# A step's piece between the two score pairs of its unit, in a fused attention kernel

## The chip, the cores and the metric

The kernel runs on one core of a Trainium2 chip. The metric is the device time of one execution in microseconds. The kernel before was run three times: 4042.91, 4030.77 and 4035.91 us, median 4035.91 us. One further execution was profiled.

## The reference

The input x has 4 batches of 2048 tokens of 256 features. Per batch:

```
h = layernorm(x) * (1 + ca) + sa
q, k = h @ Wq.T, h @ Wk.T            # 32 score heads of 8 features
v = h @ Wv.T                         # 16 value heads of 16 features
aw = softmax(q k^T * 8**-0.5)        # 32 heads, each 2048 x 2048
attn = (aw[even head] - lam * aw[odd head]) @ v
attn = rmsnorm(attn) * subln_w * (1 - LAMBDA_INIT)
x = x + ga * (attn @ Wo.T)
h = layernorm(x) * (1 + cb) + sb
x = x + gb * (h @ (ternary weight * scale).T)
```

Every element of every softmax has to go through one exponential: 4 x 32 x 2048 x 2048 of them. They are the bulk of the work.

## The kernel before

**The main loop.** It has 16 bodies, four per batch. A body covers 8 score heads (two groups of four) over all 2048 queries, in 128 units. A unit is one block of 128 keys against 512 queries for the four heads of a group. Sixteen units (all key blocks) make a segment, so a body has 8 segments. The loop has 2048 units.

**A unit on each engine.** TensorE computes the scores of a unit in two pairs of heads, numbers n = 2u and 2u+1 (`scores`, line 730). A pair is two matmuls, each with 64 contraction rows in one half of the array and 128 x 512 results, into one of three slots of two PSUM banks (`SLOTS = 3`). Before it, TensorE waits until ScalarE has finished the exponentials of pair n-3, which held the slot. ScalarE runs one ACTIVATE (Exp) of 128x1024 per pair (line 630), and does nothing else in the main loop. Two units later (`LAG = 2`) TensorE multiplies the exponentials with the values (`weighted`, line 744): four fp32 matmuls side by side in column tiles 32 wide, all 128 rows, shown in the trace as x8. They accumulate in one bank over the 16 units of a segment.

**Behind a segment.** VectorE transposes that bank into SBUF (line 994), then normalises the result in a chain of small instructions with a power by GpSimd in the middle (line 604). The first `weighted` of the next segment waits until the transpose has read the bank (`pv_read`).

**Steps and pieces.** The projections before the attention (kind "a", 8 steps for 512 tokens), the output projection and the second layer behind it (kind "e", 6 steps) and the bounds of the softmax ("m") of other batches are threaded through the units of a body, by a table that `steps_of` makes by hand. A step of kind a or e is cut into four pieces, one piece in a unit. A piece is four column-tiled fp32 matmuls, 128 columns each where it transposes (line 650) or 256 columns each where it projects (lines 656 and 664). `spread` puts the four pieces of a step in units 1, 3, 5 and 7 of a half segment, so a run of steps has a piece in every second unit. `close` puts them in four units in a row. All steps share one PSUM bank (`aux`). So the first piece of a step waits until VectorE has evacuated the step before it, and some wait for more: step 2 of kind e waits for `e_normed`, the normalised rows that VectorE (with a power on GpSimd) makes from steps 0 and 1; step 0 of kind e waits for its loads (`e_loaded`).

**Order on TensorE.** It executes in program order. In every unit it issues the scores of pair 2u, those of pair 2u+1, the weighted sum of unit u-2, and then, if the table has one, the piece.

**The tables by size.** Bodies 0 to 3 (batch 0) have the 8 steps of kind a only. Bodies 4 to 11 also have the 6 steps of kind e. Bodies 3, 7 and 11, the last of their batch, use close runs from segment 3 on (`A_TURN`, `E_TURN`, `M_TURN`); all else in bodies 0 to 11 is spread. Bodies 12 and 13 have two jobs of kind e each, spread. Body 15 has 14 steps of kind e, all close (`E_LAST`). After the main loop 10 steps of kind e are done whole.

Of the kernel before, what the change touches and what calls it, by code (L numbers as in the profile page):

```python
# [37 lines left out]
def adaln_diff_attention(nc, x, wqT, wkT, wvT, woT, lq1, lk1, lq2, lk2, subln, wfT, cT, wmod, out):  # L38
# [11 lines left out]
    PAIRS = 2  # L50
# [24 lines left out]
    A_STEPS, E_STEPS = 8, 6  # L75


    PIECES = 4
# [3 lines left out]
    M_STEPS = M_BOUNDS + NC + 1  # L82
# [59 lines left out]
    DMA = 16  # L142
# [8 lines left out]
    with ExitStack() as ctx:  # L151
# [105 lines left out]
        aux = ps[:, 7, :]  # L257
# [21 lines left out]
        a_normed = sem("a_normed")  # L279
        a_product = sem("a_product")  # L280
        a_evacuated = sem("a_evacuated")
# [352 lines left out]
        def _(pe):  # L634
# [70 lines left out]
            def m_step(m, i, bank=aux):  # L705

                if i == 0:
                    pe.wait_ge(m_open, m + 1)
                if i < M_BOUNDS:
                    for blk in range(M_BLOCKS * i, min(M_BLOCKS * (i + 1), NB)):  # L710
                        for c in range(EC):
                            at = (blk % M_BLOCKS) * (NS * BOX) + c * (NS // EC) * BOX
                            for sign in range(2):
                                last = nc.tensor.matmul(bank[:, at:at + (NS // EC) * BOX], q_sign[:, c, sign, blk * P:(blk + 1) * P],
                                                        box_w[:, c, sign, :, :].rearrange("p h k -> p (h k)"), start=(sign == 0), stop=(sign == 1))
                elif i < CRIT:
                    pe.wait_ge(m_split_done, m + 1)
                    last = m_transposes(i - M_BOUNDS, bank)
                else:
                    pe.wait_ge(m_crit_done, m + 1)  # L720
                    last = nc.tensor.transpose(bank[0:1, 0:P], m_crit[:, 0:1], ident[:, :])
                last.then_inc(m_product, 1)

            def scores(body, u, n):

                (buf, tc), blk = place_of(body, u // NB), u % NB
                pe.wait_ge(exp_done, body * (2 * BODY) + n + 1)
                for half in range(2):
                    at = 64 * half
                    last = nc.tensor.matmul(slots[slot_of(body, n)][:, half, :], keys[buf][at:at + KS_ROWS, n % PAIRS, blk * P:(blk + 1) * P],  # L730
                                            queries[buf][at:at + KS_ROWS, n % PAIRS, tc * CH:(tc + 1) * CH], start=True, stop=True)
                last.then_inc(scores_ready, 1)

            def weighted(body, u):
# [10 lines left out]
                                                start=(blk == 0), stop=(blk == NB - 1))  # L745
                last.then_inc(pv_done, 1)

            for tc in range(NC):
                for i in range(A_STEPS):
                    if i == 0:  # L750
                        pe.wait_ge(a_normed, tc + 1)
                    elif i == 2:
                        pe.wait_ge(a_evacuated, tc * A_STEPS + 2)
                    for p in range(PIECES):
                        last = a_piece(i, p, ps[:, i, :])
                    last.then_inc(a_product, 1)
# [7 lines left out]
            for b in range(B):  # L764
                pe.wait_ge(m_flag_set, b + 1)
                exact = pe.value_load(m_flag[0:1, 0:1], min_val=0, max_val=1)
                pe.reg_mov(behind, 1)
                with pe.If(exact > 0):

                    if b > 0:  # L770
                        for u in range(BODY - LAG, BODY):
                            weighted(b * GP - 1, u)
                    pe.reg_mov(behind, 0)

                    runs = pe.snap(exact_runs, min_val=0, max_val=B - 1)
                    pe.wait_ge(m_evacuated, (b + 1) * M_STEPS)
                    pe.wait_ge(pv_read, b * (GP * SEGS) + 1)
                    with pe.Fori(0, NG) as g:
                        pe.wait_ge(m_rows_loaded, (runs * EXACT_LOADS + (g + 1) * ROW_LOADS) * DMA)
                        for n in range(4 * NB):  # L780
                            head, blk = n // NB, n % NB
                            pair, at = head // 2, 64 * (head % 2)
                            pe.wait_ge(m_reduced, (runs * NG + g) * (4 * NB) + n + 1)
                            for k in range(NC):
                                last = nc.tensor.matmul(ps[:, 4 * (n % 2) + k, :], queries[0][at:at + KQ, pair, blk * P:(blk + 1) * P],
                                                        keys[0][at:at + KQ, pair, k * CH:(k + 1) * CH], start=True, stop=True)
                            last.then_inc(m_scores, 1)
                    wait_alone(pe, m_reduced, (runs + 1) * NG * (4 * NB) + 2, pe_passed)
                    wait_alone(pe, exact_split, runs + 1, pe_passed)
                    for k in range(NC):  # L790
                        if k > 0:
                            pe.wait_ge(exact_evacuated, runs * NC + k)
                        m_transposes(k, aux).then_inc(exact_product, 1)
                    wait_alone(pe, exact_evacuated, (runs + 1) * NC, pe_passed)
                    wait_alone(pe, m_rows_loaded, (runs + 1) * (EXACT_LOADS * DMA), pe_passed)
                    pe.reg_add(exact_runs, exact_runs, 1)

                for gp in range(GP):
                    body = b * GP + gp
                    steps, before = steps_of(body), None  # L800
                    for u in range(BODY):
                        if u % NB == 0 and place_of(body, u // NB)[1] == 0:
                            pe.wait_ge(group_loaded[place_of(body, u // NB)[0]], (body + 1) * (GROUP_LOADS * DMA))
                        for n in (PAIRS * u, PAIRS * u + 1):
                            scores(body, u, n)
                        if u >= LAG:
                            weighted(body, u - LAG)
                        elif gp > 0:
                            weighted(body - 1, BODY - LAG + u)
                        elif b > 0:  # L810
                            with pe.If(pe.snap(behind, min_val=0, max_val=1) > 0):
                                weighted(body - 1, BODY - LAG + u)
                        if u not in steps:
                            continue
                        kind, job, i, p = steps[u]
                        if before and (kind == "m" or p == 0):

                            bkind, bjob, bi = before
                            if bkind == "a":
                                pe.wait_ge(a_evacuated, bjob * A_STEPS + bi + 1)  # L820
                            elif bkind == "e":
                                pe.wait_ge(e_evacuated, bjob * E_STEPS + bi + 1)
                            else:
                                pe.wait_ge(m_evacuated, bjob * M_STEPS + bi + 1)
                        before = (kind, job, i)
                        if kind == "m":
                            m_step(job, i)
                        elif kind == "a":
                            if i == 0 and p == 0:
                                pe.wait_ge(a_normed, job + 1)  # L830
                            elif i == 2 and p == 0:
                                pe.wait_ge(a_evacuated, job * A_STEPS + 2)
                            last = a_piece(i, p, aux)
                            if p == PIECES - 1:
                                last.then_inc(a_product, 1)
                        else:
                            if i == 0 and p == 0:
                                pe.wait_ge(e_evacuated, job * E_STEPS)
                                pe.wait_ge(e_loaded, (job + 1) * 3 * DMA)
                            elif i == 2 and p == 0:  # L840
                                pe.wait_ge(e_normed, job + 1)
                            elif i == 4 and p == 0:
                                pe.wait_ge(e_evacuated, job * E_STEPS + 4)
                            last = e_piece(i, p, aux)
                            if p == PIECES - 1:
                                last.then_inc(e_product, 1)
            for u in range(BODY - LAG, BODY):
                weighted(B * GP - 1, u)

# [313 lines left out]
```

## Time and profile before

| | us |
|---|---|
| median of three runs | 4035.91 |
| the profiled execution | 4034.29 |
| its span, from the first to the last instruction | 4032.6 |
| ScalarE busy in the span | 3783.3 (94%) |
| TensorE busy in the span | 3766.2 (93%) |
| VectorE busy | 1199.4 (30%) |
| GpSimd busy | 635.7 (16%) |

The granted TensorE clock is 0.98 of full speed as a mean over the span. A busy share of TensorE counts modelled ends of matmuls, which overlap the next instruction, so it overstates the engine's load; the starts of instructions are the safer reading.

### The profile page before, as it was taken

The page shows a single profiled execution, that of the slowest core. Times are in us where ns is not written, and L with a number is a line of the kernel's source. Part 1 is how long each engine was busy: PE and PEld are TensorE (multiplying, and loading weights), DVE is VectorE, ACT ScalarE, POOL GpSimd, SP SyncE. Part 2 cuts the span into 40 slices and gives each one's busy share as a digit, 9 for nine tenths or more (in the row PEclk, how much of TensorE's full clock was granted, in tenths as well). Part 3 has the DMA queues.
Part 4 walks back from the last instruction along what each step waited for, and adds up shares of the span by engine and source line. Part 5 has one row for each costly group of instructions (what it writes and reads, how often), then busy time and mean ns, then how long its engine had stood idle before and what let it go on. Part 6 is the DMA issues. An engine that isn't in the chain of part 4 may idle for free.

```text
span 4032.6 us, 75553 instructions
## 1 busy us (share of the span) xinstructions
PE 3766.2 (93%) x32082; PEld 944.9 (23%) x32082; DVE 1199.4 (30%) x2778; ACT 3783.3 (94%) x4132; POOL 635.7 (16%) x402
## 2 busy tenths in 40 slices
PE   6599999999999999999999999999999999999897
PEld 3122212222222222222222222222222222211122
DVE  7222322223332323233323232232332222211134
ACT  1599999999999999999999999999999999999895
POOL 4111211111121211212012121211201001001011
PEclk8799999999999999999999999999999999999999
DMA  3402121210232323023231222222012220211101
GB/s 127 86 25 34 36 41 36 44 29 25 35 53 40 53 37 48 29 35 51 43 48 29 43 40 46 47 44 45 25 34 37 41 40 14 43 19 25 35 19 40
DMA packets 113773, 163.25 MB, mean 40 GB/s; under 512 B 19012, under 2 KB 88388, under 8 KB 113224
## 3 DMA queue, kind: packets, MB, share of 16 engines
q1 hardware_dynamic: 113416, 158.19, 21.3%
q8 instruction: 260, 4.26, 0.5%
q14 instruction: 97, 0.79, 0.1%
HBM read 97.82 MB, written 60.32 MB: 39 GB/s over the span
## 4 chain that ended last, share of the span: by engine, by line
ACT 50%; issue 22%; PE 20%; DVE 3%; DMA 2%; SPq 1%; POOL 1%; POOLq 0%; DVEq 0%; ACTq 0%
ACT probs L630 50%; PE ps L744 10%; PE ps L730 6%; PE ps L656 2%; PE ps L664 1%; SPq L383 1%; DMA queries<-m_scr 1%; DVE normed L872 1%; DVE stats L861 0%; PE ps L650 0%; POOL seg_rs L604 0%; DMA e_x<-in_x_dram 0%; POOL e_rstd L580 0%; DVE e_tmp L980 0%; DMA m_scr<-wmod_sb 0%
## 5 line engine op out<-in xcount | busy, mean ns | idle before, releaser
L630 ACT ACTIVATE probs<-ps 128x1024 f32<-128x1024 f32 x4096 | 3762.6, 1452 | 112.6 <-PE ps L730 111.4
L744 PE MATMUL ps<-probs,values 128*32 128x512 f32 x16384 | 2195.8, 608 | 7.9 <-DVE seg_t L994 3.1
L730 PE MATMUL ps<-queries,keys 64*128 64x512 bf16 x8192 | 1465.8, 387 | 142.2 <-DMA queries<-m_scr 44.0
L604 POOL TENSOR_TENSOR seg_rs<-seg_ms,neg_half 64x16 f32<-64x16 f32 x128 | 370.4, 2894 | 2967.6 <-DVE seg_ms L1003 2967.6
L730 PEld LDWEIGHTS ps<-queries,keys 64*128 64x128 bf16 x8192 | 370.5, 93 | 1874.8 <-ACT probs L630 1575.7
L744 PEld LDWEIGHTS ps<-probs,values 128*32 128x32 f32 x16384 | 323.1, 108 | 588.1 <-issue 516.4
L994 DVE STREAM_TRANSPOSE seg_t<-ps 128x512 f32<-128x512 f32 x128 | 91.8, 717 | 902.6 <-PE ps L744 902.6
L980 DVE TENSOR_TENSOR e_tmp<-ps,e_gate 128x512 f32<-128x512 f32 x64 | 44.1, 689 | 468.0 <-PE ps L656 468.0
L1007 DVE TENSOR_TENSOR seg_n<-seg_d,seg_rs 64x256 f32<-64x256 f32 x128 | 62.8, 490 | 386.5 <-POOL seg_rs L604 386.5
L957 DVE TENSOR_SCALAR a_qk<-ps 128x512 f32<-128x512 f32 x64 | 44.2, 691 | 347.5 <-PE ps L664 347.2
L650 PE MATMUL ps<-ident,normed 128*32 128x128 f32 x2048 | 99.4, 284 | 49.9 <-DVE normed L872 38.7
L1011 DVE SCALAR_TENSOR_TENSOR seg_a<-seg_n,subln_sb 32x256 f32<-32x256 f32 x256 | 133.8, 523 | 6.1
L650 PEld LDWEIGHTS ps<-ident,normed 128*32 128x32 f32 x2048 | 66.9, 114 | 180.8 <-issue 179.3
L656 PE MATMUL ps<-w_o,e_attn 128*32 128x256 f32 x1024 | 79.3, 387 | 17.8 <-DVE e_x L981 13.4
L955 DVE TENSOR_SCALAR a_hT<-ps,a_cols 128x512 f32<-128x512 f32 x32 | 25.6, 808 | 227.6 <-PE ps L650 221.5
L664 PE MATMUL ps<-a_hT,w_q 128*32 128x256 f32 x1024 | 80.1, 409 | 11.9 <-DVE a_hT L955 11.9
L1015 DVE STREAM_TRANSPOSE seg_o<-seg_a 32x512 f32<-32x512 f32 x128 | 89.5, 700 | 4.4
L656 PE MATMUL ps<-w_f,e_hT 128*32 128x256 f32 x1024 | 77.5, 385 | 8.2 <-DVE e_hT L977 8.1
L977 DVE TENSOR_SCALAR e_hT<-ps,e_cols 128x512 f32<-128x512 f32 x32 | 25.9, 808 | 178.4 <-PE ps L650 178.4
L664 PE MATMUL ps<-a_hT,w_k 128*32 128x256 f32 x1024 | 73.5, 379 | 0.0
L656 PE MATMUL ps<-w_v,a_hT 128*32 128x256 f32 x1024 | 73.5, 379 | 0.0
L960 DVE COPY a_v<-ps 128x256 f32<-128x256 f32 x64 | 23.7, 416 | 154.9 <-PE ps L656 154.6
(116 smaller groups left out, 1173.9 us busy)
## 6 DMA issues: line engine op xcount, KB each, us to landing
queries<-q_scr SPq DMA_DIRECT2D x384, 64.0 KB
keys<-k_scr SPq DMA_DIRECT2D x384, 64.0 KB
v_scr<-a_v SPq DMA_DIRECT2D x128, 128.0 KB, 2.0
values<-v_scr SPq DMA_DIRECT2D x32, 512.0 KB
q_scr<-a_parts SPq DMA_DIRECT2D x32, 384.0 KB, 2.6
k_scr<-a_parts SPq DMA_DIRECT2D x32, 384.0 KB, 2.6
a_x<-in_x_dram SPq DMA_DIRECT2D x16, 512.0 KB, 18.1
attn_scr<-seg_o SPq DMA_DIRECT2D x128, 64.0 KB, 1.6
```

What stands on the lines that cost most here:

```text
L604: nc.gpsimd.tensor_tensor(seg_rs[:, :], seg_ms[:, :], neg_half[0:64, :], ALU.pow).then_inc(seg_rs_done, 1)
L630: nc.scalar.activation(probs[:, u % PRING, n % PAIRS, :, :], slots[slot_of(body, n)], ACT.Exp).then_inc(exp_done, 1)
L650: last = nc.tensor.matmul(bank[j:j + 32, n * P:(n + 1) * P], src[:, n, c * P + j:c * P + j + 32], ident[:, :], start=True, stop=True)
L656: last = nc.tensor.matmul(bank[j:j + 32, (n % 2) * E:(n % 2 + 1) * E], hT[:, c, n * P + j:n * P + j + 32], w[:, c, :], start=(c == 0), sto ...
L664: last = nc.tensor.matmul(bank[j:j + 32, t], w[:, c, f * P + j:f * P + j + 32], hT[:, c, t], start=(c == 0), stop=(c == EC - 1))
L730: last = nc.tensor.matmul(slots[slot_of(body, n)][:, half, :], keys[buf][at:at + KS_ROWS, n % PAIRS, blk * P:(blk + 1) * P], queries[buf][ ...
L744: last = nc.tensor.matmul(pv[j:j + VW, :], values[buf][:, blk, half, :], probs[:, u % PRING, pair, half, :], start=(blk == 0), stop=(blk = ...
L957: last = V.tensor_scalar(a_qk[:, i - 2, :], bank, SCALING if i < 4 else 1.0, None, ALU.mult)
L994: V.transpose(seg_t[:, :, :].rearrange("p c d -> p (c d)"), pv).then_inc(pv_read, 1)
L1007: V.tensor_tensor(seg_n[:, :, :], seg_d[:, :, :], seg_rs[:, :].rearrange("p (c o) -> p c o", o=1).broadcast_to([64, NQ, VD]), ALU.mult).th ...
L1011: last = V.scalar_tensor_tensor(seg_a[:, :, h * VD:(h + 1) * VD], seg_n[q, :, :], 1.0 - LAMBDA_INIT, subln_sb[q, :].rearrange("p (o d) -> ...
L1015: V.transpose(seg_o[:, :], seg_a[:, :, :].rearrange("p c d -> p (c d)")).then_inc(seg_done, 1)
```

## The change

In a unit that has a piece, the order on TensorE becomes: scores of pair 2u, the piece, scores of pair 2u+1, weighted sum of unit u-2. The waits that stood ahead of a piece go with it. The tables, the semaphores and their values, and the programs of all other engines stay as they are. The waits and matmuls of a piece are moved into a function `piece`, unchanged.

```
+            def piece(step, before):
+                kind, job, i, p = step
+                if before and (kind == "m" or p == 0):
...
+                        pe.wait_ge(e_evacuated, bjob * E_STEPS + bi + 1)
...
+                if kind == "m":
+                    m_step(job, i)
+                elif kind == "a":
...
+                    last = a_piece(i, p, aux)
...
+                else:
...
+                    elif i == 2 and p == 0:
+                        pe.wait_ge(e_normed, job + 1)
...
+                    last = e_piece(i, p, aux)
...
+                return kind, job, i
...
                     for u in range(BODY):
...
-                        for n in (PAIRS * u, PAIRS * u + 1):
-                            scores(body, u, n)
+                        scores(body, u, PAIRS * u)
+                        if u in steps:
+                            before = piece(steps[u], before)
+                        scores(body, u, PAIRS * u + 1)
                         if u >= LAG:
                             weighted(body, u - LAG)
...
-                        if u not in steps:
-                            continue
-                        kind, job, i, p = steps[u]
...
```

## Rows read from the trace of the kernel before

**Rows 1.** The page: busy time, share of the span and instructions per engine.
```profile
PE 3766.2 (93%) x32082; PEld 944.9 (23%) x32082; DVE 1199.4 (30%) x2778; ACT 3783.3 (94%) x4132; POOL 635.7 (16%) x402
```
**Rows 2.** ScalarE by time: start, length, instruction, count, idle before and its releaser.
```profile
150.28 939.40 ACT L630 ACTIVATE probs<-ps 128x1024 f32<-128x1024 f32 x1024 [35.41 <-PE ps L730]
...
1260.32 234.77 ACT L630 ACTIVATE probs<-ps 128x1024 f32<-128x1024 f32 x256 [2.44 <-PE ps L730]
1497.75 1.94 ACT L630 ACTIVATE probs<-ps 128x1024 f32<-128x1024 f32 x2 [2.65 <-PE ps L730]
1500.57 232.94 ACT L630 ACTIVATE probs<-ps 128x1024 f32<-128x1024 f32 x254 [0.89 <-PE ps L730]
...
1939.41 1.94 ACT L630 ACTIVATE probs<-ps 128x1024 f32<-128x1024 f32 x2 [7.42 <-PE ps L730]
...
3068.91 1.94 ACT L630 ACTIVATE probs<-ps 128x1024 f32<-128x1024 f32 x2 [3.23 <-PE ps L730]
```
**Rows 3.** The waits by engine, ScalarE for scores: us in total, times, longest.
```profile
ACT probs L630 <- PE ps L730: 111.4, 40, 35.4
```
**Rows 4.** Order of time, weight loads: a plain unit, ScalarE setting the pace.
```profile
1254.80 0.10 PEld L730 LDWEIGHTS ps<-queries,keys 64*128 64x128 bf16 x2 [0.84 <-ACT probs L630]
...
1255.18 0.10 PEld L730 LDWEIGHTS ps<-queries,keys 64*128 64x128 bf16 x2 [0.29 <-ACT probs L630]
...
1255.51 0.16 PEld L744 LDWEIGHTS ps<-probs,values 128*32 128x32 f32 x8 [0.23 <-issue]
```
**Rows 5.** Order of time, matmuls: a close run's last piece, then plain units.
```profile
1945.03 0.61 PE L656 MATMUL ps<-w_o,e_attn 128*32 128x256 f32 x8
1945.58 0.60 PE L730 MATMUL ps<-queries,keys 64*128 64x512 bf16 x4
1946.11 1.06 PE L744 MATMUL ps<-probs,values 128*32 128x512 f32 x8
1947.11 0.60 PE L730 MATMUL ps<-queries,keys 64*128 64x512 bf16 x4
```
**Rows 6.** Order of time: eight pieces in eight units, body 15.
```profile
3890.49 1.07 PE L744 MATMUL ps<-probs,values 128*32 128x512 f32 x8
...
3891.38 0.61 PE L656 MATMUL ps<-w_f,e_hT 128*32 128x256 f32 x8
...
3893.60 0.64 PE L656 MATMUL ps<-w_f,e_hT 128*32 128x256 f32 x8
...
3894.17 0.61 PE L730 MATMUL ps<-queries,keys 64*128 64x512 bf16 x4
...
3894.61 3.90 ACT L630 ACTIVATE probs<-ps 128x1024 f32<-128x1024 f32 x4 [0.30 <-PE ps L730]
```
**Rows 7.** Order of time, first units of body 0: a piece straight behind scores.
```profile
151.36 0.10 PEld L730 LDWEIGHTS ps<-queries,keys 64*128 64x128 bf16 x2 [1.18 <-ACT probs L630]
...
151.90 0.20 PEld L650 LDWEIGHTS ps<-ident,normed 128*32 128x32 f32 x8 [0.44 <-issue]
...
152.48 0.10 PEld L730 LDWEIGHTS ps<-queries,keys 64*128 64x128 bf16 x2 [0.38 <-ACT probs L630]
```
**Rows 8.** Order of time: a segment's end, the weighted sum waits for VectorE's transpose.
```profile
1926.48 0.16 PEld L744 LDWEIGHTS ps<-probs,values 128*32 128x32 f32 x8 [0.42 <-ACT probs L630]
...
1928.46 0.16 PEld L744 LDWEIGHTS ps<-probs,values 128*32 128x32 f32 x8 [0.87 <-DVE seg_t L994]
```
**Rows 9.** Order of time: step 2 of kind e waits for the normalised rows.
```profile
1259.50 0.19 PEld L650 LDWEIGHTS ps<-ident,normed 128*32 128x32 f32 x8 [3.84 <-issue]
...
1259.88 0.11 PEld L730 LDWEIGHTS ps<-queries,keys 64*128 64x128 bf16 x4 [0.20 <-issue]
```
**Rows 10.** The waits again, TensorE for the normalised rows.
```profile
PE ps L650 <- DVE normed L872: 38.7, 12, 6.3
```
**Rows 11.** Order of time: step 1 of kind e waits in body 7.
```profile
1937.75 1.08 PE L656 MATMUL ps<-w_o,e_attn 128*32 128x256 f32 x8 [6.69 <-DVE e_x L981]
...
1938.76 1.04 PE L730 MATMUL ps<-queries,keys 64*128 64x512 bf16 x4
```

More of the change, by code:

```diff
@@ L746, in weighted @@
                 last.then_inc(pv_done, 1)
+            def piece(step, before):
+                kind, job, i, p = step
+                if before and (kind == "m" or p == 0):
+                    bkind, bjob, bi = before
+                    if bkind == "a":
+                        pe.wait_ge(a_evacuated, bjob * A_STEPS + bi + 1)
+                    elif bkind == "e":
+                        pe.wait_ge(e_evacuated, bjob * E_STEPS + bi + 1)
+                    else:
+                        pe.wait_ge(m_evacuated, bjob * M_STEPS + bi + 1)
+                if kind == "m":
+                    m_step(job, i)
+                elif kind == "a":
+                    if i == 0 and p == 0:
+                        pe.wait_ge(a_normed, job + 1)
+                    elif i == 2 and p == 0:
+                        pe.wait_ge(a_evacuated, job * A_STEPS + 2)
+                    last = a_piece(i, p, aux)
+                    if p == PIECES - 1:
+                        last.then_inc(a_product, 1)
+                else:
+                    if i == 0 and p == 0:
+                        pe.wait_ge(e_evacuated, job * E_STEPS)
+                        pe.wait_ge(e_loaded, (job + 1) * 3 * DMA)
+                    elif i == 2 and p == 0:
+                        pe.wait_ge(e_normed, job + 1)
+                    elif i == 4 and p == 0:
+                        pe.wait_ge(e_evacuated, job * E_STEPS + 4)
+                    last = e_piece(i, p, aux)
+                    if p == PIECES - 1:
+                        last.then_inc(e_product, 1)
+                return kind, job, i
             for tc in range(NC):
@@ L812, in _ @@
                                 weighted(body - 1, BODY - LAG + u)
-                        if u not in steps:
-                            continue
-                        kind, job, i, p = steps[u]
[L816 to L846, printed above, removed]
             for u in range(BODY - LAG, BODY):
```

## The prediction

> **What bounds the kernel now.** I read the page first: ScalarE is busy 94% of the span, TensorE 93% [rows 1]. That leaves open which one sets the pace, so the second view was ScalarE in order of time. The first four bodies are one unbroken row: 1024 exponentials in 939.40 us, 0.917 us each [rows 2], or 1.835 us a unit. ScalarE is the bound there, with no gap. In the whole trace it waited 111.4 us for scores, 40 times, 35.4 of it before the loop [rows 3], so 76 us in the loop. The span is the prelude (150 us), 4096 x 0.917 = 3757 us of exponentials, these 76 us, some 7 us in small losses at restarts, and a tail of about 43 us. So the time changes only by what ScalarE idles more or less. The third view was TensorE in order of time, read by the starts of its instructions, to see how near it is to ScalarE's pace.
>
> **What TensorE's orders cost.** With S for a score pair, W for a weighted sum, P for a piece of 256 columns, start to start at the full clock:
> - S to W, one pair: 0.33 us [rows 4]. Two pairs to W: 0.53 [rows 5]. So S followed by S costs 0.20, S followed by something else 0.33.
> - W to S 1.00 [rows 5], W to P 0.89 [rows 6], P to S 0.55 [rows 5].
> - S to P occurs in the trace only in the first unit with a piece, where no weighted sum stands between, at half the clock: 0.54 [rows 7]. A pair alone would be 2 x 0.20 = 0.40 there, so the change of kind costs 0.14, as 0.33 - 0.20 = 0.13 does at full clock. I take S to P as 0.33.
>
> A plain unit is then 0.53 + 1.00 = 1.53. A unit with a piece was S S W P = 0.53 + 0.89 + 0.55 = 1.97. In the new order S P S W it is 0.33 + 0.55 + 0.33 + 1.00 = 2.21. The matmuls are the same; 0.24 us is added because scores and fp32 column-tiled work alternate four times in a unit in place of twice. For a piece of 128 columns, P to S is 0.33 to 0.38 [rows 9], some 0.2 less, so 2.0 after.
>
> The Trainium skill has a rule that says the same: in "TensorEngine Tiling (Array Packing)", section Tiling Modes, a change of tiling mode (not of tile) drains the array. Scores are 64x128 tiles, W and P 128x32. It gives no figure. By the rule alone the change is a loss of two drains for each piece; the trace agrees, with 0.13 and 0.11 us (W to S against W to P).
>
> **Where it bites.** In spread runs a piece unit and a plain one alternate: before, 1.97 + 1.53 = 3.50 us against ScalarE's 3.67, room to spare; after, 2.21 + 1.53 = 3.74, 0.07 too slow. In close runs each unit falls behind by 2.21 - 1.835 = 0.375 us, before by 0.13. Lateness builds up first. Call it the time by which a pair starts after its release, the end of the exponential three before it (0.04 later). The pair must start 0.44 before ScalarE can take it [rows 6], a lone exponential takes 1.02 (two take 1.94 [rows 2]) in place of 0.917, so ScalarE loses nothing up to a lateness of 1.83 - 0.44 - 0.10 - 0.04 = 1.25. Check on the kernel before: through eight pieces in a row the lateness is 0.40 + 0.44 + 4 x 0.13 = 1.36 behind the fifth, plus 0.25 because this piece came 2.22 after the last in place of 1.97 (it waits for an evacuation): 0.36 over. ScalarE idles 0.30 there [rows 6].
>
> In plain units W of one unit ends 0.33 + 1.00 = 1.33 behind a release, so the next first pair is 0.40 late and the second 0. After the change a piece turns a first pair's lateness a into a - 0.03 for the second, a + 0.375 for the next unit's first; a plain unit takes back 0.31 (the second pair never below 0).
>
> A second cost is at segment ends. The first W of a segment starts at least 1.98 after the last W of the one before (it waits for the transpose [rows 8]). Before, the piece lay between those two (1.97), at no cost. After, the piece is ahead of the first of them, W to W is 1.53, and 0.45 is waited in addition.
>
> **Spread runs of 256 columns.** In the first segment lateness starts at 0.40 + 0.375 and the boundary adds 0.07 + 0.45: 0.05 over the limit, then six more pieces at 0.07: 0.47 us lost. Each further segment loses 0.45 + 8 x 0.07 = 1.01. Nine bodies have three such segments of kind a: 9 x 2.49 = 22.4. Three have two: 4.4. Kind e in six bodies has two stretches of a half segment before and one behind a boundary, 0.47 each: 5.6. Bodies 12 and 13 have 2.4 each: 4.8. Together 37 us.
>
> **Close runs.** Four pieces alone: 0.40 + 4 x 0.375 = 1.90, 0.65 over. Four behind a boundary (start 0.78) or one unit behind another run (start 0.95): 1.03 to 1.20 against 0.05 to 0.22 before, so +0.98. Eight in a row: 2.15 against 0.50. Bodies 3, 7 and 11: kind a 2 x 0.98 x 3 = 5.9; kind e and the bounds in two of them 2.9 each, 5.8. Body 15 has two alone (1.3), four of 0.98 (3.9) and two of eight (3.3): 8.5. Together 20 us.
>
> **The waits of pieces.** Ten times in spread runs (of the 12 in [rows 10]) the first piece of step 2 waits for the normalised rows, and ScalarE idles 2.44 us [rows 2, 9], or 2.65 and 0.89 more where the clock fell to half. The piece that starts that chain now runs earlier, by 0.93 us after a stretch of lateness 0.87 (it starts 0.33 behind the first pair, at 0.28 after the second's release, and was at 1.21). That is a gain of 0.93, but ScalarE has one pair less in hand at the wait: a loss of 0.917. And W of that unit now stands behind the wait, between one pair and the next: S to S is 1.33, against the 0.92 that ScalarE has work for, 0.4 lost at full clock and up to 0.6 at half. I take 0.5: 5 us. In bodies 7 and 11 step 1 waits for VectorE behind a segment's chain, which the piece doesn't start [rows 11]: nothing is gained, 0.917 and the W behind it are lost, given back in part since the second stall of 0.7 goes; with the three pieces behind it 1.8 each, 3.6 us. In body 12 the wait for a load (3.23 [rows 2]) costs 1.3 the same way. Together 10 us.
>
> VectorE gets a piece's product up to 1.4 us earlier, and that buys nothing else: its other evacuations end well ahead of the next step. The changes of batch, the load wait of body 15 and the tail have no piece in front and stay. DMA issues of SyncE and GpSimd's powers hang on segments' ends, which move with ScalarE's pace.
>
> **The sum.** 37 + 20 + 10 = 67 us on the profiled execution's 4034.3, which is 1.6 us under the median of three: 4102 us, 1.7% slower. If S to P and P to S are cheaper than I take them, by 0.04 together, the growth in spread runs is 0.03 and the sum about 45; if dearer by 0.04, it is 0.11 and the sum about 85. Had the extra alternations cost nothing (the lower bound, against [rows 5, 6]), nothing is lost but in the waits.
>
> **The rivals.**
> - *ScalarE hides it* (0.11). TensorE's pace in the new order stays at or under 3.67 us per two units, because weight loads get ahead of the other kind of work in a way that the one S-to-P place, at half clock, does not show. Then only the close runs lose, 5 to 15 us, against gains at the waits: 4030 to 4047. For it: TensorE idles about 0.2 us between the pairs of a spread unit, and the piece now stands there. Against: that idle time is ahead of a piece unit's cost of 0.24.
> - *Faster* (0.05). The piece fills the gap between the pairs, its product is early by 1.4 us (W and half a wait), and changes of kind are free. Each of ten waits shrinks by 1.44 - 0.92 = 0.52, and the second stalls at half clock (0.9, in eight of them) go, because the wait is shorter: 5 + 7 = 12 us, 4022. It decides if the extra alternation costs under 0.1 us a piece. Against it is the same 0.33 beside 0.20.
> - *Much slower* (0.06). A piece behind scores also has to load its weights first, which now are loaded under W; then a piece unit is 2.3 or more, spread runs lose 0.16 per pair of units and more, and the time is over 4140.
>
> **How the numbers follow.** The forecast has 0.78. Its own bounds, 45 to 85 us and some 15 us for how stalls chain, are 4060 to 4137, and I give that as the range, leaving out 0.2: the rivals. A change under 0.3% (12 us) cannot be told from none in this kernel. Faster 0.05 is that rival; within 0.3% is 0.11, the first one; slower is the rest, 0.84.
>
> **What would show it.** In the trace after: S to P and S to W 0.33 each in a piece unit at full clock; first pairs of pieces' units 2.21 apart in a close run; ScalarE's row of the first four bodies no longer unbroken, 939 us grown by about 10 (four bodies of 2.5, one of them close), in gaps of 0.1 to 0.5 that begin in the second segment; W behind a segment's end waiting 0.8 us in place of 0.4 in spread units. ScalarE's waits for scores go from 111 to about 170 us, in some hundreds of pieces. If the gaps are only at the old 40 places, the forecast is wrong.

## The result, and the profile after

The changed kernel takes 4123.48 us (median of 4 runs, 4120.68 to 4125.07) against 4036.68 us of the kernel before (median of 4): the ratio is 1.0214, with a 95% interval from 1.0196 to 1.0232. It is slower by 87 us. Forecast were 4102 us, 67 us slower, in a range from 4060 to 4137. The direction and the mechanism were right; the size was short by 20 us.

The first page lines of the changed kernel stand against [rows 1]:

```profile
span 4123.4 us, 75553 instructions
...
PE 3849.7 (93%) x32082; PEld 852.2 (21%) x32082; DVE 1206.7 (29%) x2778; ACT 3822.7 (93%) x4132; POOL 634.3 (15%) x402
...
PE 57%; ACT 26%; issue 9%; DVE 4%; DMA 1%; SPq 1%; POOL 1%; DVEq 0%; POOLq 0%; ACTq 0%
```

The counts of instructions are the same. The last line is the chain of work that ended last, by engine. Its line for the kernel before:

```profile
ACT 50%; issue 22%; PE 20%; DVE 3%; DMA 2%; SPq 1%; POOL 1%; POOLq 0%; DVEq 0%; ACTq 0%
```

ScalarE's share fell from 50% to 26%, and TensorE's rose from 20% to 57%. This is the clearest sign on the page that TensorE now sets the pace in long stretches. The busy shares hardly show it.

ScalarE in order of time, the first four bodies of the changed kernel, against the one unbroken row of 1024 exponentials in [rows 2]:

```profile
218.43 30.14 ACT L630 ACTIVATE probs<-ps 128x1024 f32<-128x1024 f32 x32 [0.27 <-PE ps L730]
...
455.77 30.15 ACT L630 ACTIVATE probs<-ps 128x1024 f32<-128x1024 f32 x32 [0.27 <-PE ps L730]
...
693.12 30.15 ACT L630 ACTIVATE probs<-ps 128x1024 f32<-128x1024 f32 x32 [0.27 <-PE ps L730]
...
966.84 5.68 ACT L630 ACTIVATE probs<-ps 128x1024 f32<-128x1024 f32 x6 [0.27 <-PE ps L730]
972.79 1.94 ACT L630 ACTIVATE probs<-ps 128x1024 f32<-128x1024 f32 x2 [0.27 <-PE ps L730]
```

The same row recurs every 237.34 us (455.77 - 218.43), then 237.35. In the kernel before, a body of 256 exponentials took 234.67 us by the ends of its exponentials (939.40 / 1024 x 256 = 234.85 with the start of the loop and the close runs of body 3 in it). So a body with the eight steps of kind a loses 2.68 us. The gaps of 0.27 us are small. A row of 32 takes 30.14 us where 32 x 0.917 is 29.34, so it hides other losses, each under the length at which the view breaks a row. Counted over the trace, ScalarE waited for scores 166 times in place of 40 (against [rows 3]):

```profile
ACT probs L630 <- PE ps L730: 157.0, 166, 33.6
```

TensorE in order of time, a piece unit, a plain unit and the next piece unit of a spread run in the changed kernel (columns as in [rows 4]):

```profile
207.83 0.10 PEld L730 LDWEIGHTS ps<-queries,keys 64*128 64x128 bf16 x2 [0.84 <-ACT probs L630]
...
208.15 0.16 PEld L664 LDWEIGHTS ps<-a_hT,w_q 128*32 128x32 f32 x8 [0.23 <-issue]
...
208.72 0.10 PEld L730 LDWEIGHTS ps<-queries,keys 64*128 64x128 bf16 x2 [0.41 <-ACT probs L630]
...
209.04 0.16 PEld L744 LDWEIGHTS ps<-probs,values 128*32 128x32 f32 x8 [0.23 <-issue]
...
210.03 0.12 PEld L730 LDWEIGHTS ps<-queries,keys 64*128 64x128 bf16 x4 [0.84 <-ACT probs L630]
...
211.57 0.10 PEld L730 LDWEIGHTS ps<-queries,keys 64*128 64x128 bf16 x2 [0.84 <-ACT probs L630]
...
211.89 0.16 PEld L664 LDWEIGHTS ps<-a_hT,w_k 128*32 128x32 f32 x8 [0.23 <-issue]
```

Read the starts: pair to piece 0.32, piece to pair 0.57, pair to weighted sum 0.32, weighted sum to the next pair 0.99. A piece unit is 2.20 and two units are 3.74 (211.57 - 207.83), against ScalarE's 3.67. The two pairs of the plain unit follow each other at once (x4 in one row); in [rows 4] the second had to wait for its slot. TensorE is full here.

The segment end that follows, against [rows 8]:

```profile
212.78 0.16 PEld L744 LDWEIGHTS ps<-probs,values 128*32 128x32 f32 x8 [0.23 <-issue]
...
214.02 0.72 DVE L997 STREAM_TRANSPOSE seg_t<-ps 128x512 f32<-128x512 f32 x1 [2.98 <-PE ps L744]
214.79 0.16 PEld L744 LDWEIGHTS ps<-probs,values 128*32 128x32 f32 x8 [0.90 <-DVE seg_t L997]
```

The weighted sums start 2.01 apart where TensorE alone would take 1.53. In the kernel before, the same two start 2.00 apart, but a piece lies between them, and the second waits 0.40 us in place of 0.90:

```profile
210.59 0.16 PEld L744 LDWEIGHTS ps<-probs,values 128*32 128x32 f32 x8 [0.23 <-issue]
...
212.59 0.16 PEld L744 LDWEIGHTS ps<-probs,values 128*32 128x32 f32 x8 [0.40 <-DVE seg_t L994]
```

### The profile page after: what moved, and what is told of

Same layout as the page of the kernel before. It is cut to its first block, busy times and chain, and to the rows that moved or that the text cites. A ratio compares the mean times of both kernels' runs of the same rounds, so it can differ in the third digit from the quotient of the medians.

```text
span 4123.4 us, 75553 instructions
## 1 busy us (share of the span) xinstructions
PE 3849.7 (93%) x32082; PEld 852.2 (21%) x32082; DVE 1206.7 (29%) x2778; ACT 3822.7 (93%) x4132; POOL 634.3 (15%) x402
## 4 chain that ended last, share of the span: by engine, by line
PE 57%; ACT 26%; issue 9%; DVE 4%; DMA 1%; SPq 1%; POOL 1%; DVEq 0%; POOLq 0%; ACTq 0%
PE ps L744 31%; ACT probs L630 26%; PE ps L730 17%; PE ps L656 4%; PE ps L664 3%; PE ps L650 2%; DVE seg_t L997 2%; SPq L383 1%; DMA queries<-m_scr 0%; DVE normed L875 0%; POOL seg_rs L604 0%; DVE stats L864 0%; DMA e_x<-in_x_dram 0%; SPq L353 0%; POOL e_rstd L580 0%
## 5 line engine op out<-in xcount | busy, mean ns | idle before, releaser
L630 ACT ACTIVATE probs<-ps 128x1024 f32<-128x1024 f32 x4096 | 3801.9, 1242 | 161.3 <-PE ps L730 157.0
L730 PE MATMUL ps<-queries,keys 64*128 64x512 bf16 x8192 | 1489.4, 388 | 114.4 <-DMA queries<-m_scr 39.6
L730 PEld LDWEIGHTS ps<-queries,keys 64*128 64x128 bf16 x8192 | 349.0, 93 | 2298.7 <-ACT probs L630 2112.4
L963 DVE COPY a_v<-ps 128x256 f32<-128x256 f32 x64 | 23.7, 416 | 150.3 <-PE ps L656 148.6
L650 PEld LDWEIGHTS ps<-ident,normed 128*32 128x32 f32 x2048 | 46.8, 113 | 96.8 <-issue 95.8
```

What stands on the lines that cost most here:

```text
L630: nc.scalar.activation(probs[:, u % PRING, n % PAIRS, :, :], slots[slot_of(body, n)], ACT.Exp).then_inc(exp_done, 1)
L650: last = nc.tensor.matmul(bank[j:j + 32, n * P:(n + 1) * P], src[:, n, c * P + j:c * P + j + 32], ident[:, :], start=True, stop=True)
```

## The experiments

Each was timed beside the kernel before, in four executions (seven of the first experiment, ten of the second). The kernel before had medians of 4035.82 us beside the first four, 4033.96 beside the one in close runs only and the last one, and 4038.12 beside the others; ratios are against these. The edits are shortened, and stand against the changed kernel unless the text says otherwise; `weighted(...)` stands for its three branches. "Growth" of a place is the change of the time between the ends of the same two exponentials against the trace of the kernel before. Segments of a body count from 0.

**Two alternations a unit, the piece ahead of the weighted sum.**

```
 scores(body, u, PAIRS * u)
-if u in steps: before = piece(steps[u], before)
 scores(body, u, PAIRS * u + 1)
+if u in steps: before = piece(steps[u], before)
 weighted(...)
```

> Order in a unit: both score pairs, the piece, the weighted sum. The piece is ahead of the weighted sum as in the changed kernel, but TensorE changes between scores and column-tiled work only twice a unit, as before. Theory (the two added alternations per piece cost 0.24 us and make the piece unit 2.21 us): a piece unit is 1.97 us again, spread runs need 3.50 us per two units against ScalarE's 3.67, the wait of 0.45 at segment ends is absorbed, and the time is that of the kernel before, 4037 us, within 8. Rival (the loss comes from the piece standing ahead of the weighted sum, which holds that sum up behind every wait and at segment ends): 4075 us or more.

4046.58 us, ratio 1.0026 (1.0014 to 1.0037): 11 us over the kernel before, where at most 8 were expected, and 77 under the changed kernel. In its trace the spread runs lose nothing. A piece directly ahead of a weighted sum shares its kind, so the pair-to-sum cost is paid once:

```profile
208.41 1.06 PE L744 MATMUL ps<-probs,values 128*32 128x512 f32 x8
209.41 0.77 PE L730 MATMUL ps<-queries,keys 64*128 64x512 bf16 x4
210.11 0.64 PE L664 MATMUL ps<-a_hT,w_q 128*32 128x256 f32 x8
210.57 1.04 PE L744 MATMUL ps<-probs,values 128*32 128x512 f32 x8
```

The second pair of the next unit with a piece waits for its slot again (0.29 us), so there is room. Where the 11 us lie is not shown. In the profiled run the loop is 6.8 us longer: 2.9 at the waits of pieces, between -1.2 and +2.4 each, another 2.9 at the changes of batch, and 1.0 elsewhere; its first exponential also comes 3.4 us later.

**Two alternations, the piece between the pairs.**

```
 scores(body, u, PAIRS * u)
+weighted(...)
 if u in steps: before = piece(steps[u], before)
 scores(body, u, PAIRS * u + 1)
-weighted(...)
```

> Order: first pair, weighted sum, piece, second pair. The piece stands between the two pairs, with two alternations a unit. Theory of alternations: a piece unit is 1.97 us; only the waits of pieces cost more, since ScalarE has one pair less in hand there: ten waits and three others by 0.7 to 0.9 each, so 4037 + 10 = 4047 us, within 10. Rival (what costs is the place between the pairs, since it delays the second pair and takes the depth of the ring of slots): as slow as the changed kernel, 4110 to 4130 us.

4041.81 us, ratio 1.0011 (1.0000 to 1.0021). The piece stands between the two pairs exactly as in the changed kernel, and the loss is gone. The place between the pairs is not what costs. The unit is first pair and last pair with one stretch of column-tiled work between them:

```profile
207.78 1.06 PE L744 MATMUL ps<-probs,values 128*32 128x512 f32 x8
208.66 0.61 PE L664 MATMUL ps<-a_hT,w_k 128*32 128x256 f32 x8
209.21 0.61 PE L730 MATMUL ps<-queries,keys 64*128 64x512 bf16 x4
```

**Four alternations, the piece last.**

```
 scores(body, u, PAIRS * u)
+weighted(...)
-if u in steps: before = piece(steps[u], before)
 scores(body, u, PAIRS * u + 1)
-weighted(...)
+if u in steps: before = piece(steps[u], before)
```

> Order: first pair, weighted sum, second pair, piece. The piece is again last in the unit, behind both pairs, but there are four alternations in a unit with a piece; plain units keep two per unit, as the second pair of one and the first of the next are adjacent. Theory of alternations: 2.21 us a piece unit; a spread run falls behind by 0.07 us per two units as in the changed kernel, close runs by 0.375 a unit. No added wait at segment ends (piece and pair lie between the two weighted sums, 2.21 against 1.98) and no pair less at the waits. So half of the loss: about 4075 us (4060 to 4090). Rival of the place between the pairs, or ahead of the weighted sum: no loss, 4037 us.

4095.79 us, ratio 1.0146 (1.0125 to 1.0167): 60 us slower than before, 6 over the range expected. The piece is at its old place, behind both pairs, and the kernel is slow because the work alternates:

```profile
204.73 0.39 PE L730 MATMUL ps<-queries,keys 64*128 64x512 bf16 x2
205.05 0.64 PE L664 MATMUL ps<-a_hT,w_q 128*32 128x256 f32 x8
205.62 0.39 PE L730 MATMUL ps<-queries,keys 64*128 64x512 bf16 x2
205.94 1.07 PE L744 MATMUL ps<-probs,values 128*32 128x512 f32 x8
206.94 0.61 PE L730 MATMUL ps<-queries,keys 64*128 64x512 bf16 x4
207.47 1.06 PE L744 MATMUL ps<-probs,values 128*32 128x512 f32 x8
208.47 0.39 PE L730 MATMUL ps<-queries,keys 64*128 64x512 bf16 x2
```

Two units take 3.74 us (208.47 - 204.73), as in the changed kernel. A full spread segment grows by 0.61 us here and by 1.08 there. The difference is the segment end, which this order passes with a piece and a pair between the two sums. The close runs lose nearly as much as in the changed kernel (from its segment 2 on body 15 grows by 9.5 us here and by 10.7 there), so more than the expected half of the loss is left.

**The segment ends alone.**

```
 scores(body, u, PAIRS * u)
-if u in steps:
+if u in steps and u % NB != 1:
     before = piece(steps[u], before)
 scores(body, u, PAIRS * u + 1)
 weighted(...)
+if u in steps and u % NB == 1:
+    before = piece(steps[u], before)
```

> The changed kernel, but the piece in the second unit of a segment stays behind the weighted sum, as before (one of eight pieces of a spread segment). Theory: this piece costs 1.97 in place of 2.21 and lies between the last weighted sum of a segment and the first of the next, so the added wait of 0.45 for the transpose goes. Per spread segment 0.45 + 0.24 of the 1.08 us go, so later segments lose 0.3 to 0.4 each, and much of that fits under the limit of lateness: 4123 - 34 = 4090 us (4083 to 4098). Rival (the segment ends cost nothing; only the pieces' number counts): one of eight pieces less, 4123 - 8 = 4115 us.

4093.06 us, ratio 1.0133 (1.0110 to 1.0155): 30 us less than the changed kernel for 76 of 761 pieces, one of the eight of a spread segment. The full segments grow by 0.41 in place of 1.08. So a segment end, together with the piece beside it, carries about a third of the loss. Of the 0.67 us a segment, 0.24 are that piece's own alternations by their price, and some 0.43 the wait; the experiment does not part the two, but the third one does (0.61 in place of 1.08, with the alternations kept).

**No wait at step 2, in both orders.** The first changes the kernel before, the second the changed one.

```
 def put(kind, job, tables):
     for i, units in enumerate(tables):
+        if kind == "e" and i == 2 and units[3] - units[0] == 6:
+            units = [units[0] + 2, units[0] + 3, units[0] + 4, units[3]]
```

> The order of the kernel before, and the spread table of step 2 of kind e moved: its four pieces in units 3, 4, 5 and 7 of its half segment in place of 1, 3, 5 and 7, so that its first piece comes 3.67 us later than the 2.96 us that it waits now for the normalised rows. Ten stalls of ScalarE (33 us in the trace of the kernel before, 2.44 to 4.4 each) go; nothing else waits in their place: 4037 - 31 = 4005 us (4000 to 4012). Rival (the stalls overlap other waits that take their place): over 4020 us.

> The changed kernel with the same moved table. Theory of two separate terms: of the changed kernel's 87 us, some 11 lie at these ten waits, the rest in TensorE's added alternations and in the segment ends; with no such wait the difference between the two orders is 87 - 11 = 76 us, so 4005 + 76 = 4081 us (4074 to 4090). Rival (the alternations cost so much only because the stalls leave TensorE late): the difference shrinks well below 76, under 4065 us.

The old order: 4000.86 us, ratio 0.9912 (0.9894 to 0.9930), 37 us faster than before. The new one: 4080.35 us, ratio 1.0106 (1.0088 to 1.0124). The difference between the orders is 79 us without the ten waits and 87 with them. So the ten waits carry 8 us of the loss, and the bulk is independent of them.

**The waiting pieces stay behind.** The changed kernel with eighteen pieces at their old place: the thirteen that the expectation names, and five more that meet the same condition (step 2 of kind e in bodies 7 and 11 and twice in body 15, and the second step 0 of body 12).

```
+late = u in steps and steps[u][0] == "e" and steps[u][3] == 0 and (steps[u][2] == 2
+    or (steps[u][2] == 1 and gp == GP - 1 and b < B - 1) or (steps[u][2] == 0 and body == (B - 1) * GP))
-if u in steps:
+if u in steps and not late:
     before = piece(steps[u], before)
 scores(body, u, PAIRS * u + 1)
 weighted(...)
+if late:
+    before = piece(steps[u], before)
```

> The changed kernel, but thirteen pieces stay behind the weighted sum: the first of step 2 of kind e (with the wait for the normalised rows), the first of step 1 in bodies 7 and 11, and the first of body 12. If the change costs at waits because ScalarE has a pair less in hand and a weighted sum stands between the next pairs, while the chain behind step 1 begins earlier, these pieces now gain from the early start and lose nothing: ten waits shorter by 0.93 than in the kernel before, and three as before. 4123 - 11 - 9 - 6 - 1 = 4096 us (4088 to 4104). Rival (the early start of the chain gains nothing): 4106 us or more.

4095.49 us, ratio 1.0140 (1.0119 to 1.0160), 28 us under the changed kernel. Moving 18 of 761 pieces back returns a third of the loss: where a piece waits, the second pair and the weighted sum belong ahead of it. What the other five did was not tested apart. The gain stands in the trace at the waits themselves: in five of the six spread bodies 4 to 10 the segment with the wait grew by -0.4 to -0.2, of which some 0.6 to 0.7 is the cost of its other pieces. So those waits are about 0.9 us shorter than in the kernel before.

**The changed order in close runs only.**

```
-if u in steps:
+late = u in steps and not (body == LAST or (gp == GP - 1 and b < B - 1 and u >= 3 * NB))
+if u in steps and not late:
     before = piece(steps[u], before)
 scores(body, u, PAIRS * u + 1)
 weighted(...)
+if late:
+    before = piece(steps[u], before)
```

> The changed order only in the close runs: body 15, and bodies 3, 7 and 11 from their segment 3 on. All spread runs keep the old order. From the segments' durations in the two traces these places carry 2.1 + 8.6 + 9.1 + 10.4 = 30 us of the loss, if segments add up: 4037 + 30 = 4067 us (4060 to 4074). Rival (the loss is in the spread runs, since they hold most of the pieces, 512 of 761, and close runs are brief): under 4052 us.

4069.53 us against 4033.96, ratio 1.0090 (1.0073 to 1.0107), 36 us, 5 more than the segments gave. The pieces in these places are 161 of 761, a fifth, and not the 249 that the expectation's 512 spread pieces leave. In the profiled run the places grew by 29 us (31 in the changed kernel), a third of the loss. So segments add up here. The median is not as clean a measure: in that run the unchanged places of the loop were 9 us shorter, at waits and changes of batch, and the first exponential came 8.6 us later.

**A faster kernel.** The old order, step 2 late as above, and step 0 of kind e one unit earlier in bodies 7 and 11 (body 3 shares the table, but has no kind e). The edit against the kernel before:

```
-    E_TURN = [close(3 * NB + 13), ...
+    E_TURN = [close(3 * NB + 12), ...
```

> The kernel before with step 2 of kind e in units 3, 4, 5 and 7, and in bodies 3, 7 and 11 the close run of step 0 of kind e one unit earlier (units 60 to 63 in place of 61 to 64), so that VectorE evacuates it ahead of its work on segment 3, not behind. The two stalls of 7.4 us and what follows them (17.6 us together) go as well: 4005 - 16 = 3989 us (3984 to 3996), faster than both kernels. Rival: the evacuation only changes places with the segment's chain and something else becomes late, over 4000 us.

3986.55 us (3979.25 to 3988.38), ratio 0.9865 (0.9848 to 0.9883): 1.3% faster than the kernel before. Nearly all the stalls of ScalarE that are left are changes of batch and waits for loads. Three of its rows in order of time:

```profile
1097.37 1.94 ACT L632 ACTIVATE probs<-ps 128x1024 f32<-128x1024 f32 x2 [2.70 <-PE ps L732]
1100.04 938.58 ACT L632 ACTIVATE probs<-ps 128x1024 f32<-128x1024 f32 x1022 [0.73 <-PE ps L732]
2041.10 1.94 ACT L632 ACTIVATE probs<-ps 128x1024 f32<-128x1024 f32 x2 [2.49 <-PE ps L732]
```

The second row is four bodies without a break: 1022 exponentials in 938.58 us, 0.918 each. The kernel before had eight gaps there.

**The same tables with the piece between the pairs,** in the order of the second experiment.

> The faster tables of e8_best with the order first pair, weighted sum, piece, second pair. If two alternations a unit are all that matters once no piece waits, the place between the pairs is neutral: 3987 us, within 6 of e8_best. Rival (between the pairs the second pair is up to 0.85 us late in a spread unit and over 1.2 in close runs, which loses in body 15's eight in a row): 3995 us or more.

3981.57 us (3977.63 to 3985.87), ratio 0.9868 (0.9851 to 0.9885) against its own runs of before. The two orders can't be told apart: 1.3% faster each.

## Why the prediction was right, and where it was short

**What bounds the kernel.** Right. In a stream ScalarE's exponentials still take 0.917 us each. The loop grew by 89.8 us between its first and last exponential in the profiled runs: 50.5 show as idle time of ScalarE, and 39.3 as busy time, where an exponential behind a gap takes 1.02 and not 0.917. The chain now runs mostly over TensorE. Of the signs named, ScalarE's waits came to 157.0 us (about 170 forecast), but 166 times in place of some hundreds; most of the losses, some 0.08 us at a piece, are too short for the view to count. The first four bodies grew by 12.6 us (about 10 forecast).

**The cost of the order.** Right: 2.21 was forecast for a piece unit, 2.20 to 2.21 measured, 3.74 for two units, 3.74 measured. The one pair-to-piece start at half the clock [rows 7] had given the right value for full clock: 0.33 taken, 0.32 measured. Had the alternations been free, the third experiment would be at the time of before; it is 60 us over. The drain at a change of tiling mode, which the Trainium skill ("TensorEngine Tiling (Array Packing)", Tiling Modes) states without a figure, fits these starts; that the drain is the cause was not tested apart from the alternation itself, which also changes the data type.

**The first gap and the limit of lateness.** The limit of 1.25 us held. A first segment was to lose 0.47 and grew by 0.51, each further one 1.01 and grew by 1.08; a body of kind a 2.49, measured 2.68. The excess of 0.07 a segment is in part the segment end (2.01 between the sums, not 1.98) and in part the pieces, at 0.077 each where 0.07 stood. A half segment of kind e grew by 0.70 where 0.47 stood; the other one of each body lies in the segment with the wait, and 0.70 is taken for it too. Spread runs together: 37 forecast, some 44 measured.

**Close runs.** 20 forecast, 24 measured. Here is one in body 3, the changed kernel; two rows of ScalarE's a unit apart are 2.21 us apart, for 1.835 us of work:

```profile
962.31 0.64 PE L656 MATMUL ps<-w_v,a_hT 128*32 128x256 f32 x8
962.42 1.94 ACT L630 ACTIVATE probs<-ps 128x1024 f32<-128x1024 f32 x2 [0.22 <-PE ps L730]
...
964.51 0.64 PE L656 MATMUL ps<-w_v,a_hT 128*32 128x256 f32 x8
964.63 1.94 ACT L630 ACTIVATE probs<-ps 128x1024 f32<-128x1024 f32 x2 [0.27 <-PE ps L730]
```

In body 15 the segments 2, 3 and 5 grew by 0.66, 0.84 and 1.95 us, where 0.65, 0.98 and 1.96 were worked out. Segment 4 grew by 1.90 where 1.65 stood, and segment 6 by 2.10 where 0.65 stood. In segment 6 eight pieces of 128 columns run in a row ahead of the four of 256, and the working left them out, though by its own prices each such unit is 2.0 us against 1.835 and adds lateness.

**The waits of pieces: the term that was mis-sized.** "I take 0.5: 5 us" for the ten waits, 3.6 for two in bodies 7 and 11, 1.3 for one. From the growth of the segments, less their share of spread runs, they took 11.3, 6.2 and 1.8: 19 us in place of 10. This is the largest error of the sum. (44, 24 and 19 make 87; 2 to 3 us more in the profiled run lie at changes of batch. The pair of kernels without the ten waits puts them at 8 and not 11.3 us.) The first such wait in the changed kernel, against [rows 9]:

```profile
1276.12 0.19 PEld L650 LDWEIGHTS ps<-ident,normed 128*32 128x32 f32 x8 [3.29 <-issue]
...
1276.51 0.10 PEld L730 LDWEIGHTS ps<-queries,keys 64*128 64x128 bf16 x2 [0.20 <-issue]
...
1276.83 0.16 PEld L744 LDWEIGHTS ps<-probs,values 128*32 128x32 f32 x8 [0.23 <-issue]
...
1276.94 1.02 ACT L630 ACTIVATE probs<-ps 128x1024 f32<-128x1024 f32 x1 [2.45 <-PE ps L730]
1278.60 0.13 PEld L730 LDWEIGHTS ps<-queries,keys 64*128 64x128 bf16 x4 [1.62 <-ACT probs L630]
...
1279.26 1.94 ACT L630 ACTIVATE probs<-ps 128x1024 f32<-128x1024 f32 x2 [1.29 <-PE ps L730]
```

The idle time at the wait is 2.45, as forecast (2.44 + 0.92 - 0.93 = 2.43). But the weighted sum behind it took 1.77 us (1276.83 to 1278.60). The granted clock there was at half, after 3.02 us without a matmul, and ScalarE had one exponential to run meanwhile: 1.29 idle where 0.4 to 0.6 was taken. All ten such sums in the changed kernel ran at half the clock, for all or part of their length (1.48 to 1.87 us). In the kernel before, two of ten kept the full clock, one of them at this same place (the 1260.32 row of [rows 2]). In those two the segment grew by 2.40 us; in the other four of bodies 4 to 10, where the clock fell in both kernels, by 1.15, 1.16, 1.31 and 2.37. So part of this term seems to be the clock's fall, which the working had priced at 0.2 us more; no run tested it apart.

**The range.** It held, but with little to spare, and not for the reasons that made it wide. Its upper end stood for dearer alternations and chained stalls; the alternations cost what was forecast, and the excess came from the waits (9 us), the spread runs (7) and the close runs (4). Its lower end of 4060 is 6 us under what its own working gives (4036 + 45 - 15 = 4066).

**The rivals.** "ScalarE hides it" fell with 3.74 us per two units. "Faster" fell on the same number, but half of its mechanism is real: with the waiting pieces behind the pairs the early start of the chain gained what was expected of it (4096 expected, 4095 measured). "Much slower" needed a piece unit of 2.3; it is 2.21.

**What stays open.** Wait stalls scatter by up to 2.2 us each where nothing was changed near them (in the kernel with the changed order in close runs only, the spread bodies' segment with the wait grew by -2.2 to +1.2). The start of the loop moves as well: the first exponential came at 150.3 us in the kernel before and at 150.2 in the changed one, but at 145.0 to 158.9 in the other ten kernels, with nothing edited ahead of the loop. So a difference of under some 10 us between two of these kernels need not come from the edit. What sets the clock's fall there was not pursued. So the split of the last 10 us between waits and scatter is uncertain.

## What to carry to other kernels

Before moving matmuls into a gap of TensorE, price each neighbour pair by the starts in the trace: here scores next to scores cost 0.20 us and scores next to column-tiled fp32 work 0.32, so a piece set among scores cost 0.24 more than one set beside its own kind, and the gap it was put in was smaller than that (0.38 between the pairs of [rows 4], less 0.20, is 0.18). Compare the resulting period with the other engine's period, not busy shares: 3.50 against 3.67 had room, 3.74 had none, and a deficit of 0.07 in 3.7 us, with a wait at segment ends that had been hidden, made half of a 2% loss. Where an instruction waits, keep the work that feeds the bound engine ahead of it. Better, move the waiting one to where its input is ready: in this kernel such moves alone gave 1.3%.

## What the runs showed of the hardware

A change between 64-row bf16 scores and 32-column fp32 matmuls costs 0.11 to 0.13 us each way in start-to-start time, both where a weighted sum and where a piece follows, and about the same at half the clock (0.14, from one place). After a stall the granted clock fell in some places and not in others, in the same program. In the kernel before, behind 2.96 us without a matmul, the next weighted sum took 1.0 us in two of ten places and 1.51 to 1.87 in eight. In the changed kernel, behind 3.02 us, it took 1.48 to 1.87 in all ten. With the waiting pieces held back, behind 1.81 us, it took 1.0 in five and 1.51 to 1.87 in five.
